# Gate scores of a graph-attention and mixture-of-experts kernel from eight extra columns of two attention products

## What is computed

```python
x = x + gnn(layernorm(x), adj, W_w, W_b, a)
x = x + ffn(layernorm(x), Wg, bg, W1, b1, W2, b2)

def gnn(h, adj, W_w, W_b, a):          # one attention head over the neighbours
    Wh = h @ W_w + W_b
    e = leaky_relu((Wh @ a[:128])[:, None] + (Wh @ a[128:])[None, :], 0.2)
    return softmax(where(adj > 0, e, -9e15), axis=1) @ Wh

def ffn(x, Wg, bg, W1, b1, W2, b2):    # 8 experts, the best two for each row
    gate = x @ Wg.T + bg
    top, idx = top_k(gate, 2)
    share = softmax(top)
    return sum over the two of share * (relu(x @ W1[e].T + b1[e]) @ W2[e].T + b2[e])
```

## Time and profile before

| | |
|---|---|
| median of three executions | 450.54 us |
| span of the profiled execution | 448.6 us |
| TensorE busy | 398.9 us, 89% of the span |
| VectorE busy | 302.4 us, 67% |
| ScalarE busy | 257.1 us, 57% |
| GpSimd busy | 206.3 us, 46% |
| mean granted TensorE clock | 0.971 of full speed |

### The profile page before, as it was taken

The page is one execution under the profiler, slowest core; times in us unless marked ns, Lnnn a source line. Parts: engine busy times, 40 slices in busy tenths (PEclk is TensorE's granted clock), DMA queues, the critical chain, the costliest instruction groups (busy, mean ns, idle before and its releaser), DMA issues.

```text
span 448.6 us, 8793 instructions
## 1 busy us (share of the span) xinstructions
PE 398.9 (89%) x2525; PEld 269.1 (60%) x2525; DVE 302.4 (67%) x847; ACT 257.1 (57%) x389; POOL 206.3 (46%) x247
## 2 busy tenths in 40 slices
PE   2699999999999998979999999999896989989930
PEld 1355555455444454434467676888796989988930
DVE  5889879989967889999689973378613731111054
ACT  1788798455467646735347653566554756665610
POOL 3463421002165433258522588556885674444440
PEclk9799999999999999989999999999999999999985
DMA  6999999874869998969379866447565666555497
GB/s 222 381 385 334 340 302 317 358 301 152 297 208 335 400 387 275 367 221 303 121 274 366 255 246 198 148 152 246 193 197 190 199 205 196 195 182 196 162 322 259
DMA packets 46459, 116.45 MB, mean 260 GB/s; under 512 B 7341, under 2 KB 20146, under 8 KB 39750
## 3 DMA queue, kind: packets, MB, share of 16 engines
q1 hardware_dynamic: 38630, 101.06, 63.0%
q0 software_dynamic: 4320, 8.47, 5.6%
q10 hardware_dynamic: 3456, 6.29, 5.2%
HBM read 84.57 MB, written 13.07 MB: 218 GB/s over the span
## 4 chain that ended last, share of the span: by engine, by line
PE 52%; DVE 14%; issue 10%; SPq 9%; DMA 7%; POOL 5%; ACT 2%; DVEq 0%; POOLq 0%; ACTq 0%
PE acc L1423 38%; DVE prob L867 5%; DMA slab<-xbuf 4%; PE yt L1524 3%; SPq L524 2%; PE acc L1524 2%; SPq L513 2%; POOL ybuf L723 2%; SPq L512 2%; SPq L523 2%; DMA ybuf<-wst,dest 1%; DVE xn L959 1%; PE pj L1382 1%; POOL xbuf L707 1%; PE m L1393 1%
## 5 line engine op out<-in xcount | busy, mean ns | idle before, releaser
L1423 PE MATMUL acc<-prob,Wh 128*128 128x512 f32 (+1 forms) x576 | 240.0, 557 | 8.1 <-DVE prob L867 4.3
L867 DVE SCALAR_TENSOR_TENSOR prob<-s_bc,E_col,G_all 128x1024 f32<-128x1024 f32 (+2 forms) x160 | 169.8, 1089 | 30.8 <-PE acc L1423 20.4
L1423 PEld LDWEIGHTS acc<-prob,Wh 128*128 128x128 f32 x576 | 104.6, 193 | 104.1 <-issue 86.0
L1210 ACT ACTIVATE G_all<-adj 128x2048 bf16<-128x2048 int32 (+1 forms) x67 | 119.3, 1801 | 18.1 <-DVE prob L867 13.6
L723 POOL DMA_INDIRECT ybuf<-wst,dest x71 | 72.3, 1018 | 61.5 <-ACT wst L1282 36.4
L707 POOL DMA_INDIRECT xbuf<-xr,slot x64 | 74.9, 1170 | 50.0 <-issue 29.8
L1524 PE MATMUL acc<-wall,prob 128*128 x368 | 51.4, 284 | 0.0
L1096 DVE COPY share<-slab 128x1 f32<-128x1 f32 x45 | 6.8, 152 | 62.8 <-DMA slab<-xbuf 62.8
L1524 PEld LDWEIGHTS acc<-wall,prob 128*128 128x128 f32 x368 | 44.7, 192 | 0.8
L1272 ACT ACTIVATE prob<-hps 128x512 f32<-128x512 f32 x46 | 27.5, 597 | 7.9 <-PE hps L1508 3.4
L690 POOL TENSOR_TENSOR rstd<-ve,mhalf 128x4 f32<-128x4 f32 (+2 forms) x10 | 11.8, 1191 | 42.7 <-DVE ve L952 42.6
(11 more groups left out here) (215 smaller groups left out, 553.8 us busy)
## 6 DMA issues: line engine op xcount, KB each, us to landing
adj<-adjT SPq DMA_DIRECT2D x52, 1024.0 KB, 7.4
adj<-adjT SPq DMA_DIRECT2D x16, 768.0 KB, 6.7
s_bc<-wall SPq DMA_DIRECT2D x47, 256.0 KB
wlb<-wall SPq DMA_DIRECT2D x24, 256.0 KB, 2.3
slab<-xbuf SPq DMA_DIRECT2D x71, 65.0 KB
adj<-ybuf SPq DMA_DIRECT2D x6, 512.0 KB, 8.0
xs<-x SPq DMA_DIRECT2D x8, 256.0 KB, 9.6
wst<-wcat ACTq DMA_DIRECT2D x8, 256.0 KB, 5.0
```

The lines of the kernel that those rows point to most:

```text
L867: nc.vector.scalar_tensor_tensor(prob[n % PR][:, 0:w], c_bc[:, P * AT[g]:P * AT[g] + w], E_col[:, u:u + 1], G[m % GR][:, k * w:(k + 1) * w ...
L1210: nc.scalar.activation(G[m % GR][:, 0:w], adj_sb[m % AR][:, 0:w], ACT.Relu).then_inc(s_G, 1)
L1423: last = nc.tensor.matmul(bank[:, 0:k * P], Wh[:, u, :], prob[n % PR][:, b * P:(b + k) * P], start=(u == 0), stop=(u == TILES - 1), skip_g ...
```

## The change

The layer norm before the gate is linear apart from its row factor: with Wgc the gate weights less their column mean, the gate scores are rstd * (x1 @ Wgc) + bg, and x1 is x + (attention numerator / row sum). The kernel after takes both summands from products that it makes anyway. `project` multiplies with nine columns in place of one, which gives x's part; `through` multiplies with 137 columns in place of 129, the eight new ones being W times Wgc. So:

- parts 7, 8 and 9 lose the transposes of `xn` (TensorE), their copies (ScalarE) and the gate products (TensorE);
- VectorE scales the eight new columns of each third (`gh`) in parts 3 to 5, and makes the gate scores from three small operations in part 8 (one before, in part 10);
- everything behind the gate moves up by one part: indices and M to p 10, shares and TensorE's rank products to p 11, slots to p 12, `tiles_left` to p 13, `tile_table` to p 14, the exponential on ScalarE to p 9; the sends start one step earlier, except in the last supergroup, where the slots stay in the same turn;
- two short steps prepare the columns: `gate_weights` in turn 27 and `gate_columns` in turn 29 of TensorE, with VectorE's parts in turns 25, 28 and 30;
- at the start SyncE loads the gate weights and their last row (128 pieces of 32 bytes each) ahead of the second tile group of `x`; the wide last row of W moves behind.

```diff
-            send_at.setdefault(TILES * (g + 1) + (14 if g < SG - 1 else 8) + i * PACE[g][0] // PACE[g][1], []).append((g, i))
+            send_at.setdefault(TILES * (g + 1) + (13 if g < SG - 1 else 8) + i * PACE[g][0] // PACE[g][1], []).append((g, i))
...
-        last_parts = [(0, 1), (2, 3), (4, 5, 6), (7, 8), (9,), (10, 11), (12,), (13,), (14,), (15,)]
+        last_parts = [(0, 1), (2, 3), (4, 5, 6), (7, 8), (9,), (10,), (11,), (12,), (13,), (14,)]
...
-            sp.dma_start(wlast_bc[:, :], W[F - 1:F, :].broadcast_to([P, F])).then_inc(s_wf, 16)
+            sp.dma_start(WgT_sb[:, :], WgT).then_inc(s_we, 16)
+            sp.dma_start(wglast_bc[:, :], WgT[F - 1:F, :].broadcast_to([P, E])).then_inc(s_we, 16)
             load_x(1)
...
+            nc.vector.tensor_copy(wag[:, 0:1], wa[:, 1:2])
...
+            dve.wait_ge(s_we, 32)
+            nc.vector.tensor_tensor(wag[:, 1:GC], WgT_sb[:, :], wglast_bc[:, :], ALU.subtract).then_inc(s_wag, 1)
...
-                    ins.then_inc(s_x1, 1)
+                    nc.vector.tensor_tensor(
+                        gh[:, mine.start:mine.stop, :], third_of(q)[:, 0:len(mine), FW:TW],
+                        rden[:, mine.start:mine.stop].unsqueeze(2).broadcast_to([P, len(mine), E]),
+                        ALU.mult).then_inc(s_x1, 1)
...
+                if p == 8:
+                    if g == 0:
+                        dve.wait_ge(s_bg, 16)
+                        dve.wait_ge(s_xg, 1)
+                    link(nc.vector.tensor_tensor(gs[:, 0:nb, :], gh[:, 0:nb, :], xg[:, AT[g]:AT[g] + nb, :], ALU.add))
+                    link(nc.vector.tensor_tensor(gs[:, 0:nb, :], gs[:, 0:nb, :],
+                                                 rstd[:, 0:nb].unsqueeze(2).broadcast_to([P, nb, E]), ALU.mult))
+                    link(nc.vector.tensor_tensor(gs[:, 0:nb, :], gs[:, 0:nb, :],
+                                                 bg_bc[:, :].unsqueeze(1).broadcast_to([P, nb, E]), ALU.add))
+                    for b in range(nb):
+                        ins = nc.vector.max(m8[:, b, :], gs[:, b, :])
+                    link(ins)
+                    nc.vector.tensor_tensor(gd[:, 0:nb], m8[:, 0:nb, 1], m8[:, 0:nb, 0], ALU.subtract).then_inc(s_gd, 1)
...
-                if p in (7, 8):
-                    h = p - 7
-                    pe.wait_ge(s_xn, 2 * g + h + 1)
...
-                        last = nc.tensor.transpose(m1[:, i * P:(i + 1) * P], xn[:, b, :], ident[:, :])
-                    last.then_inc(s_xtp, 1)
-                if p == 9:
...
-                        last = nc.tensor.matmul(m1[:, b * E:(b + 1) * E], xnT[:, b * P:(b + 1) * P], WgT_sb[:, :],
-                                                start=True, stop=True)
-                    last.then_inc(s_gate, 1)
-                if p == 12:
+                if p == 11:
                     pe.wait_ge(s_M, g + 1)
...
-                    last = nc.tensor.matmul(pj[:, GT * i + b:GT * i + b + 1], hT_of(i)[:, b * P:(b + 1) * P],
-                                            wa[:, 1:2], start=True, stop=True)
+                    at = (GT * i + b) * GC
+                    last = nc.tensor.matmul(pj[:, at:at + GC], hT_of(i)[:, b * P:(b + 1) * P], wag[:, :],
+                                            start=True, stop=True)
...
+            def gate_weights():
+
+                pe.wait_ge(s_wx, 1)
+                nc.tensor.transpose(yt[:, 0, 0:P], Wx[:, 0:F], ident[:, :])
+                nc.tensor.matmul(yt[:, 1, 0:E], ones[:, :], WgT_sb[:, :], start=True, stop=True).then_inc(s_wxt, 1)
+
+            def gate_columns():
+
+                pe.wait_ge(s_wgc, 1)
+                nc.tensor.matmul(yt[:, 1, E:2 * E], WxT[:, :], Wgc[:, :], start=True, stop=True).then_inc(s_wxg, 1)
```

More of the change, by code:

```diff
@@ L28, in build @@
     FW = F + 1
+    GC = 1 + E
+    TW = FW + E
     EPS = 1e-5
@@ L306, in third_of, with projected_col @@
         def third_of(q):
-            return (m1 if q == 1 else pj)[:, 0:3 * FW].rearrange("p (b f) -> p b f", f=FW)
+            return (m1 if q == 1 else pj)[:, 0:3 * TW].rearrange("p (b f) -> p b f", f=TW)
+        def projected_col(tiles, c):
+            return pj[:, 0:TILES * GC].rearrange("p (u c) -> p u c", c=GC)[:, tiles, c]
         s_wa = sem("s_wa")
@@ L313, in build @@
         s_wx = sem("s_wx")
+        s_wag = sem("s_wag")
+        s_wxt = sem("s_wxt")
+        s_wgc = sem("s_wgc")
+        s_wxg = sem("s_wxg")
+        s_xg = sem("s_xg")
         s_we = sem("s_we")
+        s_bg = sem("s_bg")
         s_w2 = sem("s_w2")
@@ L362, in build @@
         s_dup = sem("s_dup")
-        s_gate = sem("s_gate")
         s_gd = sem("s_gd")
@@ L807, in keep_Wh @@
                 if general:
-                    nc.vector.tensor_copy(t_col[:, tiles], pj[:, tiles])
+                    nc.vector.tensor_copy(t_col[:, tiles], projected_col(tiles, 0))
                 nc.vector.tensor_tensor(Wh[:, tiles, :], Wh[:, tiles, :],
@@ L955, in finish @@
                     dve.wait_ge(s_rstd, GROUPS + 2 * g + h + 1)
-                    if h == 0 and g:
-                        dve.wait_ge(s_xtp, 2 * g)
                     for b in half(g, h):
@@ L1009, in finish @@
                     nc.vector.tensor_copy(slot[:, :, 0:nb], slotf[:, :, 0:nb]).then_inc(s_slot, 1)
+                if p == 13 and CNT[g]:
+                    tiles_left(g)
                 if p == 14 and CNT[g]:
-                    tiles_left(g)
-                if p == 15 and CNT[g]:
                     tile_table(g)
@@ L1132, in main @@
                                                 ALU.subtract).then_inc(s_wx, 1)
+                    if n == 28:
+                        dve.wait_ge(s_wxt, 1)
+                        nc.vector.tensor_copy(WxT[:, :], yt[:, 0, 0:P])
+                        nc.vector.scalar_tensor_tensor(Wgc[:, :], yt[:, 1, 0:E], -1.0 / F, WgT_sb[:, :], op0=ALU.mult,
+                                                       op1=ALU.add).then_inc(s_wgc, 1)
+                    if n == 30:
+                        dve.wait_ge(s_wxg, 1)
+                        nc.vector.tensor_copy(Wx[:, FW:TW], yt[:, 1, E:2 * E]).then_inc(s_wx, 1)
                     for part in parts_of(n):
@@ L1244, in finish @@
             def finish(g, p):
-                if p in (7, 8):
-                    h = p - 7
-                    act.wait_ge(s_xtp, 2 * g + h + 1)
-                    ge(act, s_gate, g)
-                    bs = half(g, h)
-                    nc.scalar.activation(xnT[:, P * bs.start:P * bs.stop], m1[:, 0:P * len(bs)],
-                                         ACT.Copy).then_inc(s_xnt, 1)
                 if p == 8:
```

61 lines of the change are left out of this document (29 added, 32 removed).

## The result

The changed kernel takes **458.28 us** (median of four executions, 455.64 to 459.38) where the kernel before, beside it, takes 449.93: a ratio of **1.015, 95% interval 1.0096 to 1.0204**. It is slower, in the range of the forecast (451.0 to 457.5) by the ratio (1.015 x 450.54 = 457.3) and 0.8 us outside by the bare median. The profiled execution is the slowest of the four: span 457.6 us, 9.0 us over that of before; the medians lie 7 to 8 us apart.

The account below looks back on a forecast made before the run. It took VectorE and TensorE together as the bound from third to M, VectorE longer in supergroup 1, and SyncE's issue in the tail. Terms 0.6+0.5+0.5+0.1+3.0-0.2+1.5-1.6 = +4.4 us: span 453.0, median 454.9, range 451.0 to 457.5.

Parts of the forecast that it names:

- VectorE bounds third to M: Finish of supergroup 0: VectorE's stretch takes 21.5 us; TensorE's removed work becomes waiting, some 5 us there.
- Start: Before the first third: +0.6 us extra DMA issue, +0.5 nine columns in `project`, +0.5 column steps, +0.1 wider `through`.
- VectorE's 1.3 us in turns 25 to 30: VectorE's work for the gate columns hides in idle spells of 0.94 and 1.03 us; uncovered it would cost 1.3.
- Supergroup 0: Its finish: +1.3 us for an extra attention step less M's earlier end, +1.7 for the clock's fall; together +3.0.
- Supergroup 1: VectorE bounds up to the tile table: 1.3 us more, less 1.5 saved from the old clock fall; -0.2 us.
- after which I expect no second fall: Supergroup 1: TensorE stands only 1 to 2 us at step 83, clock stays up; otherwise +1.3 instead of -0.2.
- rival D: Worse: supergroup 1 cools twice (+1.5 us) or the 1.6 us of `pad` don't come; 456.5 us, chance 0.16.
- Supergroup 2: TensorE waits 3.5 us for M yet loses 0 by order; clock falls behind that gap, +1.5 us.
- rival A: The gap of supergroup 2 doesn't cool TensorE, so 1.5 us less: 453.4 us, chance 0.20.
- Supergroup 3 to `pad`: One weight preparation fewer and two waits gone: `pad` 1.6 us earlier, and the tail bound by SyncE's issue moves equally.
- Rival C: Faster: TensorE's removed work counts, if VectorE's stretch to M is 5 us shorter; 438 us, half 444; chance 0.12.

Follow-up runs that it names:

- filled: Changed kernel plus 36, 44, 28 and 8 idle transposes on TensorE ahead of its wait for M in supergroups 0 to 3; ratio 1.0083, run again 1.0149.
- M first: Changed kernel with VectorE making M in turn 9, ahead of the normalised rows, their low parts, packings and sends, in supergroups 0 to 3; ratio 1.0041.
- changed again: The changed kernel itself, unedited, executed and profiled a second time beside the kernel before on a slower chip; ratio 1.0183.
- ranks later: Changed kernel with TensorE's rank products, VectorE's slots and the sends two turns later in supergroups 0 to 2, tile tables in the last turn; ratio 1.0182.
- tables late: Changed kernel with the tile tables of supergroups 1 and 2 in turns 21 and 22 instead of 13 and 14; ratio 1.0165.
- columns only: Kernel before plus the changed kernel's loads, added columns and the steps making them, all unused; old gate and old finish order kept; ratio 1.006.
- the fastest kernel: Changed kernel with M ahead of the normalised rows, gate columns' steps two turns later, tile tables of supergroups 1 and 2 eight turns later; ratio 0.9854.

## Why the prediction was right, and where not

**VectorE bounds third to M, and TensorE's saved work falls into its wait: right.** The waits were forecast at 5, 6, 3.5 and 1.8 us, and measured 4.85, 5.90, 3.37 and 1.16; third to the end of M 21.4 us for 21.5. Idle work of 14 us costs nothing (filled), and VectorE's order alone brings supergroup 0 from 67.5 to 62.5 us (M first).

**Start, forecast +0.6 + 0.5 + 0.5 + 0.1 = +1.7: measured +2.65, and wrongly made up.** The second tile group of `x` is not later (VectorE's statistics start at 7.37 us and at 7.53 before), so the 0.6 did not come by that way; TensorE's first attention step still starts 0.82 us later, and only 0.15 in the second profile, where the products ahead of it took less time. The step that failed is "VectorE's 1.3 us in turns 25 to 30 hides in its two idle spells before 94.53": the spells lie behind the turn in which TensorE asks. Even the kernel before ends the target weights at 80.98 us only, 1.1 us behind the 79.9 at which the changed kernel's TensorE asks in turn 27. TensorE waits 1.60 to 2.07 us for them in the nine profiles with that step in turn 27, and in three profiles (changed again, ranks later, tables late) the clock falls behind that wait, at 83 us in the windows above. VectorE's rows in the changed kernel's first profile:

```profile
77.44 2.11 DVE L887 SCALAR_TENSOR_TENSOR prob<-s_bc,E_col,G_all 128x1024 f32<-128x1024 f32 x1
...
81.23 0.14 DVE L1159 COPY Wx<-ident 128x1 f32<-128x1 f32 x1
81.29 0.28 DVE L1160 TENSOR_TENSOR Wx<-Wx,wlast_bc 127x128 f32<-127x128 f32 x1
```

**Supergroup 0, forecast +3.0: measured +2.7 and +4.0 in two executions.** The extra attention step less M's earlier end was priced at 1.3 (measured 1.1), the fall at 1.7 (measured 1.6 or 2.9).

**Supergroup 1, forecast -0.2: measured +1.6 and -0.1.** The step "after which I expect no second fall" failed in the first profile: the gap ahead of step 83 was 1.92 us, in the forecast's 1 to 2, and the clock fell behind it, half of rival D. In the second profile the low stretch at M was as long (6.8 us) but began later and reached 4.4 us behind the start of the rank products and not 3.1; TensorE came 0.6 us later to step 83, waited 1.3 us, and there was no second fall. The bound named there, VectorE up to the tile table, was right: the table moved, the stage falls to 64.5 in the changed kernel and 61.7 in that of before.

**Supergroup 2, forecast 0 + 1.5: measured +1.2 and +2.6 in two executions, for the reasons given.** The clock fell behind 3.37 us as forecast, so rival A is out. Up to the fourth expert tile the change without a fall is at -0.3 for 0, and the fall costs 1.44 us in the first execution, for 1.5, and 2.89 in the second (the rows at the filled kernel, above). The term that the forecast lacked is the longer fall.

**Supergroup 3 to `pad`, forecast -1.6: right for `pad`, not for the time.** From the third to `pad` are 18.09 us where they were 19.69, exactly 1.6 less. SyncE's queue:

```profile
315.80 9.39 SPq L512 DMA_DIRECT2D xbuf<-zrow  x8
325.92 0.36 SPq L529 DMA_DIRECT2D slab<-xbuf  x1
...
427.75 0.34 SPq L529 DMA_DIRECT2D slab<-xbuf  x1
```

The stream starts 29.22 us behind the third and not 30.35, 1.1 of the 1.6, and takes the same pace (101.83 us to its last load, 101.37 before, where the last one is at 420.28, one behind that of the earlier trace rows). The rest is lost behind the last load: 29.85 us for 28.3. That is hardly work of the change: the kernel before with later tables has 29.6 there, columns only 30.3, both on slower chips, and the one profile of before is the shortest of all fourteen at its end. From the third of supergroup 3 on the faster chips took 160.0 to 162.4 us, most in the fastest kernel. Half of its 1.5 us over the changed one is its order: `pad` stands 19.17 us behind the third and the stream starts 0.7 us later. The other half lies behind the last load (30.6 for 29.85), and its cause stays open. On the slower chips the tail is not SyncE's alone: in the second profile of the changed kernel SyncE waits 5.4 us for ScalarE's scaled rows between 330 and 440 us.

**The sum.** +4.4 was forecast, the medians say +7 to 8, at the edge of the range. The missing 3 are the wait in turn 27, for which 1.3 was named as the uncovered price and 0 taken, the second fall of supergroup 1 or the longer falls of supergroups 0 and 2, and the 1.6 us at the end. That they still fit the range is in part luck, as its upper end had room for only one of them. Rival C was wrong for the change and right as a rule: with the stretch 5 us shorter supergroup 0 is 5 us shorter than in the changed kernel, and with the tables out of the way the kernel is faster than before by 1.5%.

The Trainium skill, page "TensorE: Matmul & The Clock Gate", section on HAM oscillation, tells that waits for data between bursts make each burst start at the lower clock. The trace agrees, with 0.50 behind all three long gaps. Its remedy is to order the work so that the engine isn't left waiting; here M first takes 7.6 us off the three finishes of the changed kernel's first profile (192.8 for 200.4), and filling the gap with idle work gives back the falls alone, 1.6 or 2.9 us in supergroup 0 and 1.4 or 2.9 up to the fourth expert tile of supergroup 2.

## What to carry to other kernels

Before work is taken off a busy engine, look for the value that it waits for, or will wait for, and ask which engine makes it: what is saved ahead of such a value is won only if the value comes earlier too. If the change cuts a dependence (here the gate from the normalised rows), move what is no longer needed out of the stretch ahead of that value. A step put into another engine's program costs nothing only if the lead of the engine that feeds it is there in that very turn, and a pure order of VectorE's work (a table eight turns later) can be worth a good part of what a new algorithm brings.

## What the hardware showed

The lower clock behind one and the same gap of 4.85 us lasted 3.4 us in one execution and 6.8 in others, so that two executions of one kernel differ by 1.3 us in one stage. In turn 27 one kernel had no fall behind 1.71 us and one behind 1.94 (96.31 and 98.59 us at the third), and among its variants a gap of 2.07 us (columns only) had none where one of 1.86 (tables late) had one. An effect of 1.5 to 3 us could be read in the stages, and not in the ratio.

A VectorE instruction with two operands in SBUF ran long beside one instruction of GpSimd, where GpSimd had started first or started soon after. In the changed kernel's first profile GpSimd's timeline has

```profile
77.20 1.27 POOL L655 TENSOR_TENSOR wst<-wst,wlb 127x512 f32<-127x512 f32 x1 [8.98 <-DMA wlb<-wlast]
...
194.01 1.28 POOL L655 TENSOR_TENSOR wst<-wst,wlb 127x512 f32<-127x512 f32 x1
```

and VectorE's `prob` at 77.44 takes 2.11 us for 1.28, its eight-element `avail` at 193.88 takes 1.45 for 0.17. In the second profile that GpSimd instruction starts at 80.75, and the target weights themselves, at 80.82, take 1.34 us for 0.28; a copy with one operand at 80.76, beside the same instruction, keeps its 0.15. In columns only `prob` had been running for 0.44 us when GpSimd started: `prob` keeps its 1.28 us, GpSimd takes 1.97 for 1.27, and VectorE's next small operation 1.25 for 0.18. So about 1 us of VectorE's time falls on what it does just then, here twice on the path to a waiting TensorE. It is no price of the change: in the kernel before, two preparations from 77.14 on take 3.58 us for 2.48 beside the same GpSimd instruction. The Trainium skill, page "GPSIMD Engine Reference", section Specifications, says that GpSimd shares its SBUF interfaces with VectorE and names contention with instructions of two SBUF inputs; the three rows agree.
